# Delta-rule attention in a perceiver block: the carried state as two 64x64 blocks, its products in 64-column pieces, U and W in separate halves

## The reference, cut to what matters

```python
def step(S, inps):
    qi, ki, vi, bi = inps
    pred = jnp.einsum('bhkv,bhk->bhv', S, ki)
    S = S + bi[..., None, None] * ki[..., :, None] * (vi - pred)[..., None, :]
    o = jnp.einsum('bhkv,bhk->bhv', S, qi)
    return (S, o)
S0 = jnp.zeros((b, H, DK, DV), x.dtype)
_, o = jax.lax.scan(step, S0, (qt, kt, vt, bt))
o = rmsnorm(o, onorm_w)
return o.transpose(1, 0, 2, 3).reshape(b, t, H * DV) @ Wo
```

## Time and profile before

| | |
|---|---|
| median of 3 runs | 739.61 us (737.41 to 741.09) |
| span of the profiled execution | 738.4 us |
| TensorE matmul busy | 612.9 us, 83% of the span |
| TensorE weight loads busy | 416.1 us, 56% |
| VectorE busy | 461.9 us, 63% |
| ScalarE busy | 256.9 us, 35% |
| GpSimd busy | 96.4 us, 13% |
| mean granted TensorE clock | 0.865 of full speed |

### The profile page before, as it was taken

The page is one execution under the profiler, slowest core; times in us unless marked ns, Lnnn a source line. Parts: engine busy times, 40 slices in busy tenths (PEclk is TensorE's granted clock), DMA queues, the critical chain, the costliest instruction groups (busy, mean ns, idle before and its releaser), DMA issues.

```text
span 738.4 us, 15612 instructions
## 1 busy us (share of the span) xinstructions
PE 612.9 (83%) x6608; PEld 416.1 (56%) x6608; DVE 461.9 (63%) x1124; ACT 256.9 (35%) x555; POOL 96.4 (13%) x140
## 2 busy tenths in 40 slices
PE   2777971876899999696799879995887999999995
PEld 1534650465888867655599746873553444444442
DVE  4846495978867354837745882677566455455552
ACT  1455520654421714343443325223331222222221
POOL 2544472310000101100100010111110000000000
PEclk9888995865579999889757969997979999999998
DMA  9994013000000000000000130000022543434321
GB/s 342 305 370 189 1 25 91 0 2 2 2 3 3 4 1 1 2 1 2 1 3 2 41 144 2 2 3 1 7 58 78 128 114 95 117 85 118 98 58 28
DMA packets 19078, 46.68 MB, mean 63 GB/s; under 512 B 3809, under 2 KB 8545, under 8 KB 18753
## 3 DMA queue, kind: packets, MB, share of 16 engines
q1 hardware_dynamic: 18368, 45.43, 20.4%
q10 hardware_dynamic: 640, 0.26, 0.2%
HBM read 43.32 MB, written 2.36 MB: 62 GB/s over the span
## 4 chain that ended last, share of the span: by engine, by line
PE 63%; DVE 21%; ACT 4%; POOL 3%; DMA 3%; SPq 2%; issue 2%; DVEq 0%; POOLq 0%
PE psum L751 8%; PE psum L746 7%; PE psum L756 7%; PE psum L594 5%; PE psum L621 3%; PE psum L709 3%; PE psum L672 3%; PE psum L712 3%; PE psum L683 3%; PE psum L560 3%; PE psum L665 3%; PE psum L718 2%; SPq L408 2%; DVE yr L1288 2%; POOL rstd L951 2%
## 5 line engine op out<-in xcount | busy, mean ns | idle before, releaser
L930 ACT ACTIVATE arena<-psum 128x512 f32<-128x512 f32 x68 | 40.6, 597 | 133.4 <-PE psum L746 125.5
L1364 DVE TENSOR_TENSOR arena<-psum,arena 128x512 f32<-128x512 f32 x64 | 44.3, 692 | 62.4 <-PE psum L751 60.6
L756 PE MATMUL psum<-arena,wed_sb 128*128 128x512 f32 x128 | 67.0, 605 | 0.0
L774 ACT ACTIVATE arena<-psum 128x512 f32<-128x512 f32 x56 | 33.4, 599 | 71.8 <-PE psum L560 45.1
L1369 DVE TENSOR_TENSOR arena<-arena 128x512 f32<-128x512 f32 x64 | 44.3, 692 | 14.4 <-PE psum L756 14.3
L560 PE MATMUL psum<-arena 32*64 32x128 f32 x1024 | 43.4, 332 | 9.6 <-DVE XA L1281 5.2
L560 PEld LDWEIGHTS psum<-arena 32*64 32x64 f32 x1024 | 37.7, 168 | 15.8 <-DVE XA L1281 5.9
L950 POOL TENSOR_TENSOR ve<-ss,eps_rms 128x4 f32<-128x4 f32 x16 | 3.9, 243 | 302.5 <-ACT yr L825 213.7
L756 PEld LDWEIGHTS psum<-arena,wed_sb 128*128 128x128 f32 x128 | 24.9, 194 | 31.6 <-issue 24.3
L751 PE MATMUL psum<-yT,weu_sb 128*128 128x512 f32 x68 | 37.3, 633 | 3.9 <-DVE arena L1364 3.9
L746 PE MATMUL psum<-yT,weg_sb 128*128 128x512 f32 x68 | 37.0, 626 | 2.2 <-ACT yr L774 2.2
(11 more groups left out here) (283 smaller groups left out, 1271.1 us busy)
## 6 DMA issues: line engine op xcount, KB each, us to landing
arena<-shares SPq DMA_DIRECT2D x64, 256.0 KB, 3.9
arena<-in_ctx_t SPq DMA_DIRECT2D x16, 514.0 KB, 8.6
arena<-in_ctx_z SPq DMA_DIRECT2D x16, 512.0 KB, 10.1
XA<-in_x SPq DMA_DIRECT2D x1, 1024.0 KB, 5.0
zlast<-in_ctx_last SPq DMA_DIRECT2D x4, 256.0 KB, 17.1
X<-x_mid SPq DMA_DIRECT2D x2, 512.0 KB, 4.5
weg_sb<-in_we_gate SPq DMA_DIRECT2D x2, 512.0 KB, 6.4
weu_sb<-in_we_up SPq DMA_DIRECT2D x2, 512.0 KB, 7.5
```

Source lines behind the costliest of these rows:

```text
L756: pe.matmul(x3, wed_sb[:, (p - 1) % (NPAIR + 1), :], act_a[pr], start=(p == 0), stop=False, skip_group_check=True).then_inc(x_down[pr], 1)
L774: return act.activation(out_, in_, ACT.Copy, scale=scale)
L930: act.activation(act_g[pr], banks[4 * pr + 2 * (n % 2)], ACT.Silu).then_inc(x_silu[pr], 1)
L1364: dve.tensor_tensor(act_gu[pr], banks[4 * pr + 1], act_g[pr], ALU.mult).then_inc(x_gu[pr], 1)
```

## The change

The state of a sequence is kept as two blocks of 64 x 64, one for heads 0 to 3 and one for heads 4 to 7 (index hq; HQ = 64), and the rest of the 128 x 128 product is no longer formed. An "s" step has 16 products of 64 stationary and 64 moving columns where it had 8 of 128 and 128. Block hq of a sequence lies on partitions hq*64 to hq*64+63, so SS and the VectorE mask operation are half as wide (128 x 512); the mask is a new constant, own_head, made once by one operation of 128 x 64. A "p" step has 16 products, each over 64 rows, with 64 stationary and 64 moving columns, where it had 8 over 128 rows; block hq of the result goes to bank b0 or b1, so that VectorE's "p", still 512 elements a row, reads from both banks. W and U are stored apart in WU, W first and U behind it in two blocks of four heads, which makes ScalarE's copy of a half into two copies of 256 columns; "wt" waits for W alone, and "s" of round 1 for U.

```diff
@@ TensorE
                     elif kind == "wt":
-                        pe.wait_ge(s_ae[u], pi * 2 + 2)
+                        pe.wait_ge(s_ae[u], pi * 4 + 3)
...
                     elif kind in ("s1", "s2", "s3"):
                         c = int(kind[1])
                         if c == 1:
                             pe.wait_ge(s_wte[u], pi + 1)
+                            pe.wait_ge(s_ae[u], pi * 4 + 4)
                         else:
                             pe.wait_ge(s_u[u], pi * 3 + c - 1)
                         for jj in range(GT):
-                            for s2 in range(2):
-                                rows_ = slice(s2 * T, s2 * T + C16 * c)
-                                last = pe.matmul((b0, b1)[s2][:, jj * D:(jj + 1) * D], KH[g][rows_, jj * D:(jj + 1) * D],
-                                                 WU[g][rows_, jj * 2 * D + D:(jj + 1) * 2 * D], start=True, stop=True)
+                            for hq in range(2):
+                                for s2 in range(2):
+                                    rows_ = slice(s2 * T, s2 * T + C16 * c)
+                                    c0 = jj * D + hq * HQ
+                                    v0 = GW + (hq * GT + jj) * HQ
+                                    last = pe.matmul((b0, b1)[s2][hq * HQ:(hq + 1) * HQ, jj * HQ:(jj + 1) * HQ],
+                                                     KH[g][rows_, c0:c0 + HQ], WU[g][rows_, v0:v0 + HQ], start=True, stop=True)
                         last.then_inc(s_s[u], 1)
                     elif kind in ("p1", "p2", "p3"):
                         pe.wait_ge(s_se[u], pi * 3 + int(kind[1]))
                         for jj in range(GT):
                             for s2 in range(2):
-                                last = pe.matmul(b0[s2 * T:(s2 + 1) * T, jj * D:(jj + 1) * D],
-                                                 WT[g][:, jj * D + s2 * T:jj * D + (s2 + 1) * T],
-                                                 SS[g][:, s2 * GW + jj * D:s2 * GW + (jj + 1) * D], start=True, stop=True)
+                                for hq in range(2):
+                                    rows_ = slice(hq * HQ, (hq + 1) * HQ)
+                                    c0 = (s2 * GT + jj) * HQ
+                                    last = pe.matmul((b0, b1)[hq][s2 * T:(s2 + 1) * T, jj * HQ:(jj + 1) * HQ],
+                                                     WT[g][rows_, jj * D + s2 * T:jj * D + (s2 + 1) * T],
+                                                     SS[g][rows_, c0:c0 + HQ], start=True, stop=True)
                         last.then_inc(s_pred[u], 1)
@@ ScalarE
                         act.wait_ge(s_a[u], pi * 2 + half + 1)
-                        copy(WU[g][:, half * GW:(half + 1) * GW], (b0, b1)[half]).then_inc(s_ae[u], 1)
+                        ws, us = ((b0, b1)[half].rearrange("p (t c n) -> p t c n", t=2, c=2)[:, :, c] for c in range(2))
+                        copy(WU[g][:, half * 2 * D:(half + 1) * 2 * D].rearrange("p (t n) -> p t n", t=2), ws).then_inc(s_ae[u], 1)
+                        copy(WU[g][:, GW:2 * GW].rearrange("p (b t n) -> p t b n", b=2, t=GT)[:, half * 2:half * 2 + 2],
+                             us.rearrange("p t (b n) -> p t b n", b=2)).then_inc(s_ae[u], 1)
@@ VectorE
+            dve.tensor_tensor(own_head.rearrange("p (h e) -> p h e", e=DK), bc(head_is[:, 0:H // 2].unsqueeze(2), [P, H // 2, DK]),
+                              bc(head_is[:, H // 2:H].unsqueeze(2), [P, H // 2, DK]), ALU.add)
...
                         dve.wait_ge(s_s[u], pi * 3 + int(kind[1]))
-                        dve.tensor_tensor(SS[g].rearrange("p (n h e) -> p n h e", h=H, e=DK),
-                                          psum[:, bank * 512:(bank + 2) * 512].rearrange("p (n h e) -> p n h e", h=H, e=DK),
-                                          bc(head_is.unsqueeze(1).unsqueeze(3), [P, 2 * GT, H, DK]), ALU.mult).then_inc(s_se[u], 1)
+                        states = psum[:, bank * 512:(bank + 2) * 512].rearrange("p (b n) -> p b n", b=2)[:, :, 0:GT * HQ]
+                        dve.tensor_tensor(SS[g].rearrange("p (b j n) -> p b j n", b=2, n=HQ),
+                                          states.rearrange("p b (j n) -> p b j n", n=HQ),
+                                          bc(own_head.unsqueeze(1).unsqueeze(1), [P, 2, GT, HQ]), ALU.mult).then_inc(s_se[u], 1)
```

More of the change, by code:

```diff
@@ L24 @@
 H, DK = 8, 16
+HQ = H * DK // 2
 T = 64
@@ L234, in perceiver @@
         WU = [stage[g][:, 0:2 * GW] for g in range(NG)]
-        SS = [stage[g][:, 2 * GW:4 * GW] for g in range(NG)]
+        SS = [stage[g][:, 2 * GW:3 * GW] for g in range(NG)]
         hm = [stage[g][:, 0:3 * GW].rearrange("p (c n) -> p c n", c=3) for g in range(NG)]
@@ L253, in perceiver @@
         below = rowv[:, 2:4, :].rearrange("p i c -> p (i c)").rearrange("p (r m) -> p r m", r=C16)
-        take = carve(sb("small", [P, 192])[:, :])
+        take = carve(sb("small", [P, 256])[:, :])
         eye64, tril, tri32 = take((T,)), take((T,)), take((S,))
@@ L259, in perceiver @@
         head_is = take((H,))
+        own_head = take((HQ,))
         NH = GT * 2 * H
@@ L651, in _ @@
                     elif kind == "wt":
-                        pe.wait_ge(s_ae[u], pi * 2 + 2)
+                        pe.wait_ge(s_ae[u], pi * 4 + 3)
                         for jj in range(GT):
-                            last = pe.transpose(b0[:, jj * D:(jj + 1) * D], WU[g][:, jj * 2 * D:jj * 2 * D + D], ident[:, :])
+                            last = pe.transpose(b0[:, jj * D:(jj + 1) * D], WU[g][:, jj * D:(jj + 1) * D], ident[:, :])
                         last.then_inc(s_wt[u], 1)
@@ L681, in _ @@
                                 rows_ = slice(s2 * T, (s2 + 1) * T)
-                                c0 = t * 2 * D + D + h // 2 * 2 * DK
+                                c0 = GW + (h // 4 * GT + t) * HQ + h % 4 // 2 * 2 * DK
                                 last = pe.matmul((b0, b1)[n // 16][rows_, n % 16 * 2 * DK:(n % 16 + 1) * 2 * DK],
@@ L1320, in _ @@
                         dve.wait_ge(s_pred[u], pi * 3 + c)
-                        uu = WU[g].rearrange("p (t c n) -> p t c n", c=2, n=D)[:, :, 1, :]
-                        dve.scalar_tensor_tensor(out=uu, in0=b0.rearrange("p (t n) -> p t n", n=D), scalar=chunk[c], in1=uu,
-                                                 op0=ALU.mult, op1=ALU.add).then_inc(s_u[u], 1)
+                        uu = WU[g][:, GW:2 * GW].rearrange("p (b n) -> p b n", b=2)
+                        pred = psum[:, bank * 512:(bank + 2) * 512].rearrange("p (b n) -> p b n", b=2)[:, :, 0:GT * HQ]
+                        dve.scalar_tensor_tensor(out=uu, in0=pred, scalar=chunk[c], in1=uu, op0=ALU.mult,
+                                                 op1=ALU.add).then_inc(s_u[u], 1)
                     elif kind == "onorm":
```

## The result

The changed kernel took 723.70 us, the median of 4 runs (717.71 to 732.94), against 738.74 us (737.41 to 741.09) before. Over the ten runs of the changed kernel the median is 730.0 us, 1.2% under the 739.1 of before. The 723.70 itself is the middle between 718.83 and 728.57, and none of the four runs was near it. The forecast was 735.2 us, with a range from 731.5 to 739.7. So the sign was right, the profiled execution gained 22.5 us of span where 4.4 had been worked out, and the range did not hold the time.

A forecast was written before the change was run, and what follows sets the result against it. TensorE was taken as the bound in solves 2 and 3, waits for VectorE's mask as the gain in lone rounds; 2.1 + 1.9 + 0.2 + 0.3 = 4.5, taken as 4.4, gave 735.2 us, range 731.5 to 739.7.

The forecast's parts named there:

- TensorE's pace: "s" and "p" steps: a 64 x 64 piece costs about 30 ns, so 64 matmuls take 1.90 us.
- the prediction's own chain: Lone rounds of solves 1 and 4: one group's steps through TensorE and VectorE, 3.89 to 3.98 us, taken as 3.95.
- The sum: All four solves: gains of 2.1, 0.2, 0.3 and 1.9 us, together 4.5, taken as 4.4.
- The mask's 2.1 and 1.9 us: Solves 1 and 4: gains from three lone rounds each, 0.69 us a round, less 0.15 us in solve 4.
- The seam: Ahead of round 1: "s" starts about 0.15 us later behind ScalarE's copies, costing 0.15 us in solve 4 only.
- (a): Solve 3: the new "s" makes the clock rise earlier, 731.8 to 733.5 us; chance 0.13.
- (b): Whole kernel: shifted half-clock stretches or a gap downstream give the gain back, 738 to 740 us; chance 0.18.
- (c): "s" and "p" steps: pieces do not run abreast, 53 to 60 ns each, 771 to 781 us; chance 0.03.
- (d): Lone rounds: pieces do not hold full clock, 745 us with one of solves 1 and 4, 755 with both; chance 0.06.
- The 62 ns for each matmul: "s" and "p" steps: sequencer's time per matmul without hardware decode, 3.97 us a step, 784 us; chance inside (c).

The follow-up runs named there:

- e3: Changed kernel with its pieces reordered so that two quarters of TensorE's array take turns instead of four; 722.52 us, ratio 0.978.
- e8: Changed kernel with four pieces in a row on the same quarter of TensorE's array, in "s" and "p"; 750.57 us in one run, against 739.79.
- e2: Kernel before, with VectorE's mask made for sequence 0 only (128 x 512), TensorE's products unchanged; 729.50 us, ratio 0.987.
- e9: Changed kernel with two quarters in turn in solves 1 and 4 and four in turn in solves 2 and 3; 724.87 us, ratio 0.981.
- e1: Changed kernel with VectorE's mask over 1024 elements, as before the change; 744.87 us, ratio 1.009.
- e10: Changed kernel with extra unread products of ones behind second-group "s" and "p" steps (not the last "p") in solves 1 and 4; 722.67 us, ratio 0.976.
- e4: Changed kernel with each piece cut in two, to 32 moving columns, both halves in a row on the same quarter; 761.83 us in one run, against 739.61.
- e0: The changed kernel run again without any edit; six runs of 718.68 to 734.37 us, median 731.86, against 739.11.
- e5: e3 with both "s" pieces that stand abreast writing one PSUM bank; 721.30 us in one run.
- e7: e3 with "o" and the products into and out of the lanes turned so that row groups write different PSUM banks; 723.39 us, ratio 0.978.

## Why the prediction was wrong

**TensorE's pace** is the step that failed. It said: "Since 128 and 32 moving columns give the same pace, it is not the streaming that sets it but what the two share, the load of 64 columns." The new pieces have loads of 64 columns too, and one comes every 17.0 ns; so that load is not what holds the two rows at 30. What the prediction left out is how many places of the array follow each other: the same pieces cost 17.0, 23.3 and 40.9 ns with four quarters, two, and one (e3, e8). Nor were the neighbours like the new pieces. L560 does take four places in turn, but of 32 rows x 64 columns, not quarters, and streams 128 columns; L594 has two quarters in turn. Why L594 has 30 ns with 32 columns, where pieces of 64 in the same turn have 23.3, is open, so the equality of the two rows is not explained, only shown to say nothing of the load. With 17.0 ns the prediction's own chain gives the right round: "s" to the mask 0.76 us instead of 1.21, "p" to VectorE's start 0.77 instead of 1.23, mask and VectorE's "p" as forecast, together 3.1 us; 3.08 was measured. I bounded the pace from above only (60 ns). The side on which I was wrong had no bound, and the range did not reach it.

**The sum.** The mask's 2.1 and 1.9 us in solves 1 and 4 are right (e2: 2.18, 2.16). The pieces gave another 1.3 and 2.4 there and not nothing; solve 2 gave 3.68 and not 0.2, solve 3 4.59 and not 0.3, of the last an estimated 1.3 by the clock. With the 16.3 us of the solves in place of the 4.4 the forecast would have been 723.3 us. That this is so near the measured 723.70 is luck: the 6.2 us outside the solves and the two long runs of four stand on opposite sides. In solve 2 all of it is pace: TensorE works 4.93 us less (six steps of 0.8 to 0.9 us, at full clock before and after) and waits 1.25 us more, so a quarter of the gain was off the path at once.

**The seam.** "s" of round 1 was to start 0.15 us later. Its loads wait for the copy of the transposed W:

```profile
451.79 1.10 PEld L671 LDWEIGHTS psum<-arena,pc 16*64 16x64 f32 x64 [0.38 <-ACT pcT L783]
```

0.38 us, where the earlier trace rows has 0.17. Right, and 0.06 us too small.

**The rivals.** (a) did not come by its mechanism: the half-clock stretch around the start of solve 3 lasts 20.4 us in after and 23.9 before, but 20.4 also in e2, whose pieces are those of before. (b) fits e9's trace and, with the other sign, the first comparison, where 6.2 us of the gain lie outside the solves. (c) is excluded at four quarters in turn and true at one (e8, one run). (d) got 0.06; six of ten executions were long, with 728 to 734 us and not 745, and the one of them that was traced shows it. I had priced it with the slow pace and asked whether small pieces hold the clock, not what TensorE's idle time in a lone round would be if they were fast. The 62 ns for each matmul that the prediction takes from the Trainium skill, TensorE: Matmul & The Clock Gate, section "Wait — 56ns, not 53.3ns?", are contradicted by the new pieces (17.0 ns) still more than by L594 (30.2).

## What to carry to other kernels

Before small products are priced by a neighbour, compare how many different quarters of the array follow each other there; the same piece cost 17, 23 or 41 ns by its order alone. A price between two equal neighbours is no bound where it is not known why they are equal. Bound an unseen price on the side of a gain too. And where TensorE gets faster beside an engine that doesn't, look at what its new idle time may cost in granted clock: here a kernel with faster products and the old mask was slower than before (e1), and a filler or a slower order that kept the clock had the better median.

No version tried beats all others: e3 (722.5 us, within 3.2) and e10 (722.7) are below the changed kernel's ten-run median of 730.0, but not below its best executions (718).

## What the runs showed of the hardware

- 64 x 64 float32 pieces, per traced matmul at full clock: 17.0 ns with four quarters in turn, 23.3 with two, 40.9 with one. At half clock, 64 with four quarters take 1.92 us, 30.0 ns, less than twice the 17.0. With 32 moving columns, and each quarter asked twice before the next: 16.0 ns; in the lone rounds of that kernel TensorE stood for 1.12 us at a time without a releaser in the trace (e4).
- The clock went from full to half in lone rounds behind waits of 0.3 to 1.5 us (after, e0, e1), and once without a wait, with one quarter at work at a time (e8). Where two quarters alternated without much waiting (e3, e5 to e7, e9) or a filler ran (e10) it did not in the profiled executions. Once down it stayed for 31 to 34 us of nearly unbroken work, "o" and the products out of the lanes above all (e0, e1), though in solve 1 of after and of e0 it was back behind 3.4 us. What tells these apart is not settled.
- Open too is why "o", the products out of the lanes, and L594 keep 30 ns with two quarters in turn and 32 columns, where pieces of 64 columns take 23.3. For the first two the banks are excluded (e7). Giving "o" four quarters would be the next thing to try; it was not tried.
